# Cross-attention: VectorE adds two of a head's probability chunks, GpSimd adds the pair, and TensorE makes two sets of ones-products in place of three

## The reference

```python
q = _qdq(x) @ _qdq(wq).T + bq
kv = cond @ wkv.T + bkv
k, v = jnp.split(kv, 2, axis=-1)
...
attn = jax.nn.softmax(jnp.einsum('bnhd,bmhd->bhnm', q, k) * scale, axis=-1)
o = jnp.einsum('bhnm,bmhd->bnhd', attn, v).reshape(B, N, C)
out = _qdq(o) @ _qdq(wp).T + bp
```

## Time and profile before

| | us |
|---|---|
| median of 3 runs | 643.45 |
| lowest, highest | 641.19, 646.16 |
| profiled execution | 641.48 |
| its span, first to last instruction | 639.7 |

### The profile page before, as it was taken

One profiled execution on the slowest core, in us unless ns is written; L12 is line 12 of the kernel. 1 busy time (PEld: TensorE's weight loads), 2 busy tenths in 40 slices (PEclk: granted clock), 3 DMA queues, 4 the chain that ended last, 5 costly groups with the idle time before them and its releaser, 6 DMA issues.

```text
span 639.7 us, 12391 instructions
## 1 busy us (share of the span) xinstructions
PE 602.2 (94%) x4340; PEld 476.6 (75%) x4340; DVE 369.5 (58%) x680; ACT 299.4 (47%) x424; POOL 228.6 (36%) x120
## 2 busy tenths in 40 slices
PE   5999999999999999999999999997697999979998
PEld 3877788888887677777776777764497988769996
DVE  3796621330434778878878777766564334366652
ACT  4435232233231555555555555564247667634441
POOL 2000200000001778888788888870001544400000
PEclk9999999999999999999999999999699899979999
DMA  8664545514529655566555666600130324144510
GB/s 305 228 227 161 173 170 180 191 72 157 203 93 282 165 149 146 147 164 159 153 143 143 158 165 156 156 29 2 26 145 28 132 76 188 67 181 151 196 66 33
DMA packets 29758, 92.17 MB, mean 144 GB/s; under 512 B 5473, under 2 KB 9569, under 8 KB 23009
## 3 DMA queue, kind: packets, MB, share of 16 engines
q1 hardware_dynamic: 28480, 89.67, 45.8%
q10 hardware_dynamic: 1248, 2.10, 0.9%
HBM read 65.02 MB, written 18.35 MB: 130 GB/s over the span
## 4 chain that ended last, share of the span: by engine, by line
PE 87%; DVE 4%; ACT 3%; issue 2%; POOL 1%; DMA 1%; SPq 0%; POOLq 0%; ACTq 0%; DVEq 0%
PE ps L333 17%; PE ps L334 16%; PE ps L335 16%; PE ps L1283 11%; PE ps L1368 9%; PE ps L1380 9%; PE ps L1394 4%; POOL p_sum L574 1%; PE ps L1354 1%; PE ps L1356 1%; DMA f_ring<-stream 1%; PE ps L1549 1%; PE ps L1562 1%; ACT probs L744 1%; PE ps L1265 1%
## 5 line engine op out<-in xcount | busy, mean ns | idle before, releaser
L693 ACT ACTIVATE p_ring<-ps 128x1024 f32<-128x1024 f32 x128 | 125.7, 1022 | 103.1 <-PE ps L1368 76.2
L957 DVE TENSOR_REDUCE m_part<-ps 128x1 f32<-128x512 f32 x240 | 150.5, 684 | 30.7 <-PE ps L1283 27.9
L574 POOL TENSOR_TENSOR p_sum<-p_sum,p_ring 128x1024 f32<-128x1024 f32 x60 | 142.9, 2381 | 9.4 <-ACT p_ring L693 5.3
L1283 PE MATMUL ps<-k_stack,q_max 96*128 96x512 f32 x240 | 87.3, 424 | 1.4 <-issue 0.6
L1368 PE MATMUL ps<-q_stack,k_stack 98*128 98x256 f32 x512 | 81.5, 288 | 0.2 <-ACT p_ring L693 0.2
L1368 PEld LDWEIGHTS ps<-q_stack,k_stack 98*128 98x128 f32 x512 | 75.8, 192 | 7.8 <-ACT p_ring L693 1.2
L1380 PE MATMUL ps<-p_ring,v_head 128*32 128x256 f32 x1024 | 71.6, 383 | 0.1
L333 PE MATMUL ps<-xt_h,h_ring 128*128 128x256 f32 x208 | 60.8, 292 | 2.1 <-DVE xt_l L1071 2.1
L910 DVE SCALAR_TENSOR_TENSOR kl_buf<-ps,biases,kh_buf 128x512 fp32r<-128x512 f32 x32 | 23.9, 749 | 64.0 <-ACT kh_buf L651 63.7
L333 PE MATMUL ps<-h_ring,wkv_h 128*128 128x512 f32 x128 | 52.4, 410 | 8.2 <-DVE l_ring L870 7.2
L334 PE MATMUL ps<-xt_l,h_ring 128*128 128x256 f32 x208 | 60.1, 289 | 0.0
(11 more groups left out here) (186 smaller groups left out, 1032.4 us busy)
## 6 DMA issues: line engine op xcount, KB each, us to landing
f_ring<-stream SPq DMA_DIRECT2D x29, 1024.0 KB, 4.9
k_stack<-kh_scratch SPq DMA_DIRECT2D x60, 256.0 KB, 4.6
kh_scratch<-kh_buf SPq DMA_DIRECT2D x32, 256.0 KB, 5.5
kl_scratch<-kl_buf SPq DMA_DIRECT2D x32, 256.0 KB, 5.8
v_head<-v_all SPq DMA_DIRECT2D x16, 512.0 KB, 3.0
k_stack<-kl_scratch SPq DMA_DIRECT2D x30, 256.0 KB, 4.2
v_all<-stream SPq DMA_DIRECT2D x4, 256.0 KB, 4.6
f_ring<-stream SPq DMA_DIRECT2D x4, 256.0 KB, 5.4
```

What stands on the lines that cost most here:

```text
L574: nc.gpsimd.tensor_tensor(p_sum[:, p, :], p_ring[:, 0, :] if n == 0 else p_sum[:, p, :], p_ring[:, c % 4, :], ALU.add).then_inc(sums_done, 1)
L693: nc.scalar.activation(p_ring[:, c % 4, :], ps[:, 2 * (c % 2):2 * (c % 2) + 2, :].rearrange("p b n -> p (b n)"), ACT.Exp, scale=XSCALE).th ...
L957: nc.vector.reduce_max(m_part[:, j // NT, j % NT:j % NT + 1], maximum_bank(j), AX.X).then_inc(max_read, 1)
L1283: nc.tensor.matmul(maximum_bank(j), q_max[p][0:SPLIT_ROWS, at128(j % NT)], k_stack[p][0:SPLIT_ROWS, j // NT * D:(j // NT + 1) * D], start= ...
```

## The change

VectorE gets one more instruction a head, `add_pair`: it adds chunks 2 and 3 (slots 2 and 3 of `p_ring`) into a new tile `p_pair` of 128 x 1024, between its reads 10 and 11 of head h+1. GpSimd's second add takes `p_pair` in place of chunk 2, so `p_sum` holds chunks 0 to 6 after five adds as before. TensorE makes no ones-products of chunk 3. ScalarE's exp 6 waits for `pair_done` in place of a count of `sums_done`, and exp 7 waits for it as well. In the last head VectorE makes the pair add besides its five adds.

```diff
--- before.py
+++ after.py
@@ -44,9 +44,10 @@
 DH = D // H
 HPG = P // DH
 SPLIT_ROWS = 3 * DH
-SUM_CHUNKS = (0, 1, 2, 4, 5, 6)
+SUM_CHUNKS = (0, 1, 3, 4, 5, 6)
+IN_SUM = SUM_CHUNKS + (2,)
 NSUMS = len(SUM_CHUNKS) - 1
-SUMS_BEFORE = (-2, -1, 0, None, 1, 1, 2, None)
+SUMS_BEFORE = (-2, -1, 0, None, 1, 1, None, None)
 MAX_ROWS = 2
 MT = M // P
 CHUNKS = MT // 4
@@ -190,6 +191,7 @@
                 p_ring = sb("p_ring", [P, 4, CW], F32, b)
                 v_head.append(sb("v_head1", [P, MT, DH], F32, b))
                 p_sum = sb("p_sum", [P, 2, CW], F32, b)
+                p_pair = sb("p_pair", [P, CW], F32, b)
                 o_t = sb("o_t", [P, 2 * N], F32, b)
         with ExitStack() as cd:
             f_ring.append(sb("f_ring2", [P, KT, D], F32, cd))
@@ -268,6 +270,7 @@
         ones_set = sem("ones_set")
         vh_loaded = [sem(f"vh_loaded{i}") for i in range(2)]
         sums_done, sums_used = sem("sums_done"), sem("sums_used")
+        pair_done = sem("pair_done")
         max_done, max_read = sem("max_done"), sem("max_read")
         negm_ready, mrow_done, mrow_ready = sem("negm_ready"), sem("mrow_done"), sem("mrow_ready")
         s_done, exp_done, pv_done = sem("s_done"), sem("exp_done"), sem("pv_done")
@@ -566,13 +569,17 @@
             def sum_chunks(h, p):
 
                 for n, c in enumerate(SUM_CHUNKS[1:]):
-                    pool.wait_ge(exp_done, 8 * h + c + 1)
+                    if c == 3:
+                        pool.wait_ge(pair_done, h + 1)
+                    else:
+                        pool.wait_ge(exp_done, 8 * h + c + 1)
                     if n == 0:
                         wait(pool, sums_used, h - 1)
                     else:
                         pool.wait_ge(sums_done, NSUMS * h + n)
                     nc.gpsimd.tensor_tensor(p_sum[:, p, :], p_ring[:, 0, :] if n == 0 else p_sum[:, p, :],
-                                            p_ring[:, c % 4, :], ALU.add).then_inc(sums_done, 1)
+                                            p_pair[:] if c == 3 else p_ring[:, c % 4, :],
+                                            ALU.add).then_inc(sums_done, 1)
 
             for g in range(KT):
                 pool.wait_ge(k_stored[g], 32 * NCTX)
@@ -690,6 +697,8 @@
                     summed = SUMS_BEFORE[c]
                     if summed is not None:
                         wait(act, sums_done, NSUMS * h + summed)
+                    elif c >= 6:
+                        act.wait_ge(pair_done, h + 1)
                     nc.scalar.activation(p_ring[:, c % 4, :], ps[:, 2 * (c % 2):2 * (c % 2) + 2, :].rearrange(
                         "p b n -> p (b n)"), ACT.Exp, scale=XSCALE).then_inc(exp_done, 1)
 
@@ -1010,10 +1019,18 @@
             maximum_row(0, 0)
             chunk_maxima(1, 2, 3)
 
+            def add_pair(h):
+
+                dve.wait_ge(exp_done, 8 * h + 4)
+                wait(dve, sums_done, NSUMS * (h - 1) + 2)
+                nc.vector.tensor_tensor(p_pair[:], p_ring[:, 2, :], p_ring[:, 3, :], ALU.add).then_inc(pair_done, 1)
+
             def head(h, p, after=True):
 
                 first = isinstance(h, int) and h == 0
-                chunk_maxima(h + 1, 3, 15)
+                chunk_maxima(h + 1, 3, 11)
+                add_pair(h)
+                chunk_maxima(h + 1, 11, 15)
                 if not first:
                     normalize_output(h - 1)
                 chunk_maxima(h + 1, 15, 16)
@@ -1038,12 +1055,17 @@
             def add_last(n):
 
                 h, c = H - 1, SUM_CHUNKS[n + 1]
-                dve.wait_ge(exp_done, 8 * h + c + 1)
+                if c == 3:
+                    add_pair(h)
+                    dve.wait_ge(pair_done, h + 1)
+                else:
+                    dve.wait_ge(exp_done, 8 * h + c + 1)
                 if n == 0:
                     dve.wait_ge(sums_used, h - 1)
                 dve.wait_ge(sums_done, NSUMS * h + n)
                 nc.vector.tensor_tensor(p_sum[:, 1, :], p_ring[:, 0, :] if n == 0 else p_sum[:, 1, :],
-                                        p_ring[:, c % 4, :], ALU.add).then_inc(sums_done, 1)
+                                        p_pair[:] if c == 3 else p_ring[:, c % 4, :],
+                                        ALU.add).then_inc(sums_done, 1)
 
             add_last(0)
             add_last(1)
@@ -1379,7 +1401,7 @@
                 for k in range(4):
                     last = nc.tensor.matmul(bank(7)[k * DH:(k + 1) * DH, 0:N], v_head[p][:, 4 * c + k, :],
                                             p_ring[:, c % 4, k * N:(k + 1) * N], start=c == 0, stop=c == CHUNKS - 1)
-                if c not in SUM_CHUNKS:
+                if c not in IN_SUM:
                     last = denominators(p_ring[:, c % 4, :])
                 last.then_inc(pv_done, 1)
```

## The result

The change makes the kernel slower by about 0.7%: 645.75 us (median of 20 runs, 643.85 to 650.16) where the kernel before has 641.13 (20 runs). The ratio is 1.007, with a 95% interval of 1.0049 to 1.0092. The forecast was 647 with a range of 641.5 to 651.5, most likely within 1%.

The account below looks back on a forecast made before the run. TensorE, 94% busy, was taken as the bound, with GpSimd's chain nearly as long. Head 0 -0.4, 13 periods +2.1 and the last head +2.0 gave +3.7 us, so 647 us, range 641.5 to 651.5.

Parts of the forecast that it names:

- The saved set: Chunk 3's ones-products on TensorE: leaving them out gains 0.43 us a head in fifteen heads, if nothing else is late.
- The pair: VectorE's add of chunks 2 and 3 takes 1.22 us and starts 0.16 us behind read 10.
- TensorE's own path: TensorE's period per head goes from 14.88 to 15.03 us, less up to 0.26.
- the idle before maximum 0: TensorE's 0.26 us idle before maxima 0 and 1 in the loop, said to absorb 0 to 0.26 of the delay.
- GpSimd's loop: Ring from ones-products of `p_sum` through reads, pair and GpSimd's adds to the next: 15.04 us, setting the period, +2.1 over 13.
- Head 0: The first head: -0.4 us, with no merge there and the add hidden by a wait for ScalarE.
- The last head: +2.0 us: GpSimd's sum of head 14 about 1.1 later, then VectorE's extra add before the division.
- The size: The total change, +3.7 us, from the profiled 641.48; with the three-run median of 643.45, 647 was predicted.
- Rival 1: The merge has unseen slack and GpSimd's chain is shorter, so TensorE keeps its 0.43 a head: 639 us; chance 0.12.
- the merge's delay: Reads 11 and 12 start 0.58 us later behind the pair, all on the way to TensorE's merge; least about 0.30.
- Rival 2: The pair comes later than taken and both loops grow by all of it: 651.5 at a 0.5 gap; chance 0.15.
- Rival 3: VectorE's and GpSimd's adds meet; a hold-up of half a microsecond a head would give 653.6 us; chance 0.05.

Follow-up runs that it names:

- Run a: The kernel before with chunk 3's ones-products left out and nothing added; 635.14 us, ratio 0.9896.
- run c: The changed kernel, but GpSimd's second add takes chunk 2 at once and doesn't wait for the pair; 670.82 us, ratio 1.0423.
- run b: The kernel before with VectorE's pair add made but used by nobody, all ones-products kept; 646.61 us, ratio 1.0077.
- run f: The changed kernel with the pair add over half its width, 512 of 1024 columns; 639.05 us, ratio 0.9954.
- run g: The changed kernel with the pair add two reads later, behind read 12; 692.08 us, ratio 1.0774.
- run h: The changed kernel with the ones-products of `p_sum` moved behind scores 2 and ScalarE's output copy one exp later; 647.42 us, ratio 1.0079.
- control m: The kernel before with only the later ones-products of `p_sum` and the later output copy; 650.63 us, ratio 1.013.
- run d: The changed kernel with the last head as before: five VectorE adds, no pair, chunk 3's ones-products kept there; 647.18 us, ratio 1.008.
- run j: The changed kernel with later ones-products of `p_sum` and output copy, and heads 14 and 15 as before the change; 642.9 us, ratio 1.0022.
- run e: The changed kernel with chunks 4 and 5 as the pair, added late and taken last by GpSimd, last head as before; 678.93 us, ratio 1.0534.

## Why the prediction was right

- **The saved set, 0.43 a head: right.** Run a gives 0.44.
- **The pair, 1.22 us, 0.16 behind read 10: right in size.** It takes 1.21 to 1.23. The gap was taken too long: it is 0.05 at most, as the chain of waits of after has it (start, us, what):

```profile
316.10 0.61 DVE m_part L966
316.71 0.05 issue
316.75 1.24 DVE p_pair L1026
```

- **TensorE's own path, 15.03 less up to 0.26: mis-sized by about half a microsecond, without effect on the sum.** It is 14.50 at most (the good head of run c), and run b shows 0.09 a head for the pair where 0.32 to 0.58 was forecast. The merge waits 0.33, not 0.58, and the idle before maximum 0 gives 0.26 of it back. The step took the pair's cost on read 12 as if nothing behind it had slack. That GpSimd's ring had the same length on paper hid this: had it been shorter, the forecast would have been some 0.5 a head too slow.
- **GpSimd's loop, 15.04: right.** 15.02 in the steady heads; runs f and g move it as the sum says, and run h against its control m shows what it withholds. The base was 14.88, and 14.84 in the same ten heads, so a head costs 0.18 more where 0.16 was forecast.
- **Head 0, -0.4: not readable.** The first copy is 2.5 earlier, mostly by a clock stretch of before, and in run d, with the same head 0, it is 0.4 earlier.
- **The last head, +2.0: mis-sized, 2.7.** The wait grew by 1.20 (2.27 - 1.07) where 1.1 was forecast. From there to the last ones-products it takes 444.13 - 432.98 = 11.15 in place of 9.75, +1.40 where +0.9 was forecast. The pair's part is the forecast 0.9; the other 0.5 lies between the ones-products and exp 3, where TensorE's scores are made at 0.63 and 0.52 of the full clock. The prediction priced the idle time and not the clock behind it. Run j against run h, 4.5 us, holds a larger price, with the wait's own. That the idleness is the cause of the lower clock is inferred from their order in after and in runs b, c, d and h; it can't be its length alone, since the clock stayed at 1.00 behind the nine waits of 2.04 to 2.14 us in run g.
- **The size: partly luck.** The forecast took +3.7 from the profiled execution and laid it on 643.45, the median of three runs. Twenty runs of before have a median of 641.13, 2.3 lower, and the measured difference is 645.75 - 641.13 = +4.6. The base was too high and the change too low, and the two errors cancel in part.
- **Rival 1** (the saving is kept) fails through GpSimd's ring; the merge's delay would have left most of the saving (runs b and h). **Rival 2** did not occur, since the gap is short. **Rival 3** was right to be kept small for this kernel, yet its price of 0.5 a head was far off: where the adds meet, a head costs up to 5 us more (runs b and c).
- **Open:** why the clock fell behind some idle stretches and not behind others as long, and why after was granted 0.72 from 244 to 248 and before 0.91 from 204 to 224.

## What to carry to other kernels

An engine busy 94% of the span can be relieved of 0.44 us a head for nothing, if a helper's sum is ready only 1.08 us before it is asked for and the edit delays it by as much: add up the helper's ring, from its consumer round to its consumer, before an operation is put into it. Where VectorE and GpSimd both add two tiles in SBUF, order them by a wait, since left free the one that comes second pays for both. An idle stretch of TensorE of some two microseconds can cost more than its length (a head of run c lost five), and it need not (the steady heads of run g), so look at the granted clock behind it before it is priced.

## What the runs showed of the hardware

- **Two adds exclude each other, and the one that starts later pays.** VectorE's add of 128 x 1024 goes from 1.23 to 2.92-3.39 us when GpSimd's started 0.07 to 0.55 before it (runs b, c and e); GpSimd's goes from 2.38 to 3.33 and 3.45 when VectorE's started 0.13 and 0.01 before it (runs b and c).
- **TensorE's clock behind an idle stretch.** Idle times here are those between matmuls. Behind 2.07 us TensorE was granted 0.63 and 0.52 over four microseconds (after), behind 2.05 us 0.50 over six (run d); the ten microseconds with an idle stretch of 1.83 in them show 0.75 and 0.57 (run c), those with 1.46 show 0.70 and 0.62 (run b). But behind nine stretches of 2.04 to 2.14, one a head, it stayed at 1.00 (run g, from 301 to 454), and so it did behind 1.43 in the last head of run b, behind 0.87 (before) and behind 0.80 and 1.21 (run j). The length of the stretch alone doesn't decide it.
